# At most two gathers under way in the three edge stretches of a two-layer graph network

## The reference

```python
xl = (x @ Wl).reshape(n, H, C);  xr = (x @ Wr).reshape(n, H, C)
m = xl[src] + xr[dst];  e = jax.nn.leaky_relu(m, NEG_SLOPE)      # edges and a self loop for each node
logits = jnp.einsum('ehc,hc->eh', e, att)
...                                                              # softmax over each destination, sum, graph norm
x = _layernorm(x + elu(graph_norm(out)))
for l in range(2):
    h_src = h[src];  c = comp[l][etype]
    msg = sum(c[:, b:b+1] * (h_src @ basis[l, b]) for b in range(4))
    agg = jax.ops.segment_sum(msg, dst, num_segments=n_nodes)
    h = jnp.tanh(agg + h @ loop_w[l] + bias[l])
x = _layernorm(x + h)
```

## Time and profile before

| | value |
|---|---|
| median of three runs | 3410.07 us |
| span of the profiled execution, first to last instruction | 4033.8 us |
| time of the profiled execution outside that span | not in the profile |
| mean granted clock of TensorE | 0.917 |
| busy: PE, DVE, ACT, POOL | 80%, 58%, 45%, 51% |
| mean DMA rate over the span | 144 GB/s |

### The profile page before, as it was taken

The page is one execution under the profiler, slowest core; times in us unless marked ns, Lnnn a source line. Parts: engine busy times, 40 slices in busy tenths (PEclk is TensorE's granted clock), DMA queues, the critical chain, the costliest instruction groups (busy, mean ns, idle before and its releaser), DMA issues.

```text
span 4033.8 us, 65767 instructions
## 1 busy us (share of the span) xinstructions
PE 3226.5 (80%) x17551; PEld 2290.4 (57%) x17551; DVE 2357.5 (58%) x7747; ACT 1828.3 (45%) x4347; POOL 2055.6 (51%) x2407
## 2 busy tenths in 40 slices
PE   3778777778778758888987888887996888886887
PEld 2666656666556545557874444445884444444665
DVE  3444344444444348897875666664444666665998
ACT  1333333334334324447993444443443444444665
POOL 5555555555555502225766666661226666662555
PEclk8988888889899879999998999998998988998999
DMA  3333333334333338877972333335993333333998
GB/s 82 97 101 95 93 93 92 94 95 105 92 94 102 86 78 239 241 230 252 291 253 81 88 84 83 83 83 167 299 299 88 84 82 81 84 85 117 341 326 279
DMA packets 660630, 579.29 MB, mean 144 GB/s; under 512 B 74468, under 2 KB 535173, under 8 KB 660261
## 3 DMA queue, kind: packets, MB, share of 16 engines
q1 hardware_dynamic: 494580, 335.02, 28.5%
q0 software_dynamic: 67008, 156.44, 14.3%
q10 hardware_dynamic: 98672, 83.61, 6.3%
HBM read 366.34 MB, written 208.43 MB: 142 GB/s over the span
## 4 chain that ended last, share of the span: by engine, by line
PE 36%; issue 16%; another core or an unknown queue 13%; ACT 12%; DVE 11%; DMA 4%; ACTq 3%; SPq 2%; POOL 1%; DVEq 0%; POOLq 0%
PE bank L1073 15%; PE bank L1084 4%; ACT work L1317 3%; PE bank L1120 3%; PE bank L1127 2%; DMA work<-w_d 2%; PE bank L1064 2%; DMA w_d<-work 1%; DVE work L1927 1%; ACTq L430 1%; ACT work L1309 1%; PE bank L1140 1%; PE bank L1094 1%; DVE work L1813 1%
## 5 line engine op out<-in xcount | busy, mean ns | idle before, releaser
L1927 DVE SCALAR_TENSOR_TENSOR work<-bank,coef,work 128x128 f32<-128x128 f32 x2400 | 664.5, 343 | 490.2 <-ACT work L1351 269.3
L1073 PE MATMUL bank<-basis_s,work 128*128 128x512 f32 x1600 | 815.9, 634 | 39.4 <-issue 18.1
L785 POOL DMA_INDIRECT work<-in_x_dram,slot_src x400 | 386.0, 965 | 497.5 <-PE bank L887 345.5
L827 POOL DMA_INDIRECT work<-h_d,slot_src x400 | 393.9, 985 | 230.2 <-issue 104.9
L827 POOL DMA_INDIRECT work<-x_d,slot_src x400 | 393.3, 983 | 226.9 <-issue 107.2
L785 POOL DMA_INDIRECT work<-in_x_dram,slot_dst x400 | 386.4, 966 | 123.6 <-issue 123.6
L1073 PEld LDWEIGHTS bank<-basis_s,work 128*128 128x128 f32 x1600 | 293.8, 205 | 272.9 <-issue 242.5
L1650 DVE TENSOR_TENSOR work<-work,bank 128x512 f32<-128x512 f32 x100 | 68.8, 688 | 608.5 <-ACT bank L1200 531.2
L1351 ACT ACTIVATE work<-bank,coef 128x128 f32<-128x128 f32 x800 | 288.4, 365 | 293.5 <-PE bank L1073 147.0
L1084 PEld LDWEIGHTS bank<-work 128*126 128x126 f32 x1600 | 217.9, 203 | 290.2 <-issue 228.3
L1084 PE MATMUL bank<-work 128*126 128x128 f32 x1600 | 233.3, 293 | 171.7 <-ACT work L1357 95.4
(11 more groups left out here) (278 smaller groups left out, 7547.7 us busy)
## 6 DMA issues: line engine op xcount, KB each, us to landing
w_d<-work SPq DMA_DIRECT2D x800, 62.5 KB
work<-in_x_dram SPq DMA_DIRECT2D x194, 256.0 KB, 4.5
work<-x_d SPq DMA_DIRECT2D x194, 256.0 KB, 4.4
w_d<-work SPq DMA_DIRECT2D x400, 66.9 KB
work<-w_d SPq DMA_DIRECT2D x398, 64.0 KB, 3.4
work<-w_d ACTq DMA_DIRECT2D x390, 64.0 KB, 3.4
xl_d<-work SPq DMA_DIRECT2D x97, 256.0 KB
work<-xl_d SPq DMA_DIRECT2D x97, 256.0 KB, 3.8
```

Source lines behind the costliest of these rows:

```text
L785: pool.indirect_dma_start(quad(k, i % 3)[:, c, :], None, x, bass.IndirectOffsetOnAxis(ap=table[:, a:a + 1], axis=0)).then_inc(e_in[i % 3], 16)
L827: pool.indirect_dma_start(quad(0, i % 3)[:, c, :], None, (x1_d, h1_d)[l], bass.IndirectOffsetOnAxis(ap=slot_src[:, a:a + 1], axis=0)).then ...
L1073: pe.matmul(psum[YBANKS[k % 5]][:, :], quad(1, i % 2)[:, c, :], basis_s[:, l, :, :].rearrange("k b n -> k (b n)"), start=True, stop=True). ...
L1927: ins = dve.scalar_tensor_tensor(o, psum[YBANKS[k % 5]][:, b * D:(b + 1) * D], coef[:, i, l, c, b:b + 1], o, ALU.mult, ALU.add)
```

## The change

In all three edge stretches the gathers now count on two semaphores in turn, and GpSimd waits before each gather until the one before the last, which counts on the same semaphore, has landed. In stage 1 the two are the source and the destination gathers; in stages 4 and 6 the even and odd chains. TensorE waits for both semaphores before it turns a row. Data, buffers, the order of the gathers and the wait for a free place are as before.

```diff
-            sem("drop_out"), [sem(f"e_in{k}") for k in range(3)], [sem(f"drop_in{k}") for k in range(3)],
+            sem("drop_out"), sems("e_in"), [sem(f"drop_in{k}") for k in range(3)],
...
-            | {n: [sem(f"r_{n}{k}") for k in range(3)] for n in ("h_in", "nh_out")}
+            | {"h_in": sems("r_h_in"), "nh_out": [sem(f"r_nh_out{k}") for k in range(3)]}
...
                     for k, table in ((0, slot_src), (1, slot_dst)):
+                        after(pool, e_in[k], 16 * (CHAINS * i + c))
                         pool.indirect_dma_start(quad(k, i % 3)[:, c, :], None, x,
-                                                bass.IndirectOffsetOnAxis(ap=table[:, a:a + 1], axis=0)).then_inc(e_in[i % 3], 16)
+                                                bass.IndirectOffsetOnAxis(ap=table[:, a:a + 1], axis=0)).then_inc(e_in[k], 16)
...
-                        a = c * ROWS + i
+                        a, k = c * ROWS + i, c % 2
+                        after(pool, r["h_in"][k], was["h_in"][k] + 16 * (2 * i + c // 2))
                         pool.indirect_dma_start(quad(0, i % 3)[:, c, :], None, (x1_d, h1_d)[l],
-                                                bass.IndirectOffsetOnAxis(ap=slot_src[:, a:a + 1], axis=0)).then_inc(r["h_in"][i % 3], 16)
+                                                bass.IndirectOffsetOnAxis(ap=slot_src[:, a:a + 1], axis=0)).then_inc(r["h_in"][k], 16)
...
             def turn_edges(i):
-                pe.wait_ge(e_in[i % 3], 128 * (i // 3 + 1))
+                for k in range(2):
+                    pe.wait_ge(e_in[k], 16 * CHAINS * (i + 1))
...
                 def turn(i):
-                    pe.wait_ge(r["h_in"][i % 3], was["h_in"][i % 3] + 64 * (i // 3 + 1))
+                    for k in range(2):
+                        pe.wait_ge(r["h_in"][k], was["h_in"][k] + 32 * (i + 1))
```

More of the change, by code:

```diff
@@ L333, in counts_before @@
             with_first = {"m_ps": QUADS}
-            lists = {"h_in": [64 * len(range(k, ROWS, 3)) for k in range(3)], "w_out": [16 * ROWS] * CHAINS}
+            lists = {"h_in": [32 * ROWS] * 2, "w_out": [16 * ROWS] * CHAINS}
             lists_with_first = {
```

## The result

The changed kernel takes 4162.6 us (median of 4 runs, 4156.66 to 4172.75) against 3410.03 us: ratio 1.2216, 95% interval 1.2195 to 1.2236. That is 752.6 us slower, with a forecast of +75 us and a range that ended at 3590.

The account below looks back on a forecast made before the run. It took no engine to bound the whole alone, with gathers hidden under PE's edge rows. Stage 1's 20 us and stages 4 and 6's 64 us gave +84, rounded to +75: 3410 + 75 = 3485 us, range 3400 to 3590.

Parts of the forecast that it names:

- What that meets: Edge stretches: GpSimd's new 11.5 and 5.6 us a row set against rows of 11.7 and 5.28 us in the runs.
- The new pace: GpSimd's gathers: two take the larger of 2.50 us and landing + 0.27; quiet 2.51, beside stores 3.3 to 3.6 us.
- Landing beside stores: Gathers in stages 1 and 6: landing takes 2.85 to 3.5 us beside stores, against 2.1 to 2.25 us quiet.
- The wake-up of 0.27 us: GpSimd's unmet waits: 0.27 us from the release to the start of the next gather.
- met waits are free: GpSimd's and PE's waits: one already met costs nothing that a row shows; PE's second wait was priced at nothing.
- B: Rival: GpSimd bounds all three edge stretches at 13 and 6.5 us a row, 370 us; at half, 3595 us; chance 0.17.
- A: Rival: the wait is covered under PE's pace in the edge stretches, no change, 3405 to 3417 us; chance 0.22.
- C: Rival: stores in the edge stretches gain what the gathers give up, 41 us faster, 3369 us; chance 0.11.
- Expected views: Profile after: GpSimd waits over all gathers, its PE waits shrunk some 150 us in stage 1, PE waiting before turns.
- three signs of being wrong: Starts staying 1.25 us apart beside stores; long PE waits yet more time; shrunken waits before L1208 and L1366 with less time.

Follow-up runs that it names:

- again: The kernel before, unchanged but for a comment line, profiled again: 3411.03 us, ratio 1.0005, profiled span 3406.8 us.
- skip1: The kernel before with the gather of the fourth chain left out in stages 4 and 6: 3351.98 us, ratio 0.9827.
- rel1: The kernel before, limited to one gather under way in stages 4 and 6, stage 1 as before: 4898.14 us, ratio 1.4352.
- thin6: The changed kernel with each store of stage 6 writing 5 rows instead of 125: 4102.34 us, ratio to before 1.2014.
- swap2: The changed kernel with the two waits of a row's first gather in the other order: 4106.57 us, ratio to before 1.2026.
- edges2: The kernel before with two gathers under way in stage 1 only: 3827.07 us, ratio 1.1219.
- rel2: The kernel before with two gathers under way in stages 4 and 6 only: 3761.86 us, ratio 1.1039.
- wait2: The kernel before with one more, already met wait on each row's first gather from the fourth row on: 3412.62 us.
- met1: The kernel before with an already met wait on every gather but a row's first: 3410.93 us.
- all5: The change with five gathers under way on five semaphores, in all three edge stretches: 3426.78 us, ratio 1.0047.

## Why the prediction was wrong

- **The step that failed first: "What that meets".** It took rows of 11.7 and 5.28 us for the runs, with GpSimd's 10.0 and 5.0 under them. They are 10.25 and 5.06 us: GpSimd is the bound, with no margin at all (`again`, `skip1`), and its 760 us of added idle time are the slowdown. The 335 us of waiting for PE in the earlier trace rows belonged to the odd execution; in the second trace it is 0.6 us. The text had the numbers to see it. It assumed that the node stages shrink by up to 14% in the runs; the time outside the gathers' stretches, from first gather to last, was 1414.5 us in the first trace and 1373.7 in the second, 3% less. By the table the rest is 4034 - 2635 = 1399 us. Left as it was, this rest leaves 3410 - 1399 = 2011 us for the edge stretches, and GpSimd's back-to-back gathers alone are 1600 x 1.25 = 2000 us. Two numbers that meet so closely point at the bound. This step is worth 1.45 us a row of stage 1 and 0.22 of the others, some 190 us of the 684 by which the stretches' growth (768 us) exceeds the forecast's +84.
- **The step that failed by more: "The new pace", the right mechanism, mis-sized.** I had 11.5 and 5.6 us a row (in the sum 11.9 for stage 1: "at par" with 11.7, and 0.2 for stalls); it is 14.4 and 6.8, in all three stretches some 495 us of the 684. In stage 1 it is even over the bound of 13.2 us that I gave for all gathers beside stores. Three parts were missing: the semaphore has its count 0.3 us after the packets that I took for the landing (`rel1`), so quiet gathers pay as well (`thin6`); two under way take 0.3 us a pair more than one would, by longer landings and, it seems, by the later of two landings (`rel1`); and the first gather of a row starts 0.48 us later still, because its wait for the landing stands ahead of it (`swap2`, 56 to 65 us). How stage 1 splits into these was not measured.
- **Landing beside stores.** I had 2.85 to 3.5 us and blamed the stores for all of the loss. They lengthen the tail (to 5.3 us from 4.3) and the mean (to 2.88 us from 2.60), worth 0.5 to 0.6 us of a relational row's 1.8 (`thin6`).
- **The wake-up of 0.27 us, and that met waits are free,** held, but for a row's first gather: 0.26 us in the changed kernel, `edges2`, `rel2`, `swap2`, `thin6` and `rel1`, and `wait2` and `met1` within 0.1% of before. PE's second wait was not tried alone; `all5`, with five waits of PE a row, costs 15 us for everything together.
- **The rivals.** B, GpSimd as the bound of all three stretches, is what happened. It had 0.17, and a price of 370 us at its bound, half of the true one, as it started from rows that were too long and gave rows after of 13 and 6.5 us. A is out, as GpSimd's pace did not stay at 1.25 us a gather; C is out, as the time rose.
- **Expected views.** That GpSimd's waits would spread over all gathers held. Its waits for PE did not shrink by some 150 us but are gone, as they are in the second trace of before; and PE waits for gathers before its turns, which it did there too (226 us before L1065, where the first trace shows 32 us before L1064). None of the three signs of being wrong that I named came up: they were signs of another mechanism, not of another size. That the span would stay within 50 us of 4033.8 did not (4170.8). By accident of the first execution the two spans differ by only 3.4%, where the runs differ by 22%.
- The Trainium skill ("DMA: Bandwidth & Descriptors", Anatomy of one DMA — SWDGE path) counts its fixed 2.0 us up to the semaphore update. So the earlier trace rows, which end at the last packet, did not bear it out as I wrote. By the estimate of 2.15 us for 64 KB from that page two under way would have been free. The smallest landings here are 2.4 us by the semaphore, and the measurement decides.

## What to carry to other kernels

Before a wait or a limit is put on an engine, divide: instructions times their spacing against the measured time of the stretch, not against a profiled execution that runs 18% over the runs. An engine busy for 60% of the span by the page (7 tenths in the slices of its stretches) can be issuing without a pause, since the 0.30 us between its instructions is not counted as busy. Where the issuing engine is the bound, a limit of `n` transfers under way is free only if `n` times the issue spacing exceeds the tail of landing plus wake-up, not its median: here 4 x 1.25 = 5.0 us was still 2% too few, with a median landing of 3.4 us in stage 1.

## What the runs showed of the hardware

So the wait that comes last should be carried by the instruction itself: with the landing's wait written first in the code the kernel took 4106.57 us, with it written last 4162.6.
- The fewer gathers under way, the more PE stood waiting and the lower was TensorE's granted clock, as a share of 2.4 GHz. In stage 4 it was 0.99 before (PE busy 486 of 506 us), 0.93 in the changed kernel (520 of 684 us) and 0.77 in `rel1` (700 of 1244 us). In the changed kernel GpSimd's gathers never wait for PE, so the lower clock is not needed as a cause.
- By the semaphore a gather of 128 rows of 512 bytes lands 2.4 us after the start of GpSimd's instruction at the least. In stage 4 the median is 2.5 to 2.9 us with one to four under way and the longest 4.1 to 5.5; in stage 1, where the DMA engines are busier (54% against 38% in stage 4 in the second trace of before), the median is 2.8 to 3.4 us with two to four, and the longest 9 to 11 us.
